# Experts' stage of an attention-and-experts kernel: its batches' front work spread over three batches

## The reference, cut to what matters

```python
x = layernorm(x + (seq_out + gated * mem_val) @ out_w.T + out_b)
logits = x @ gate_w.T + gate_b                  # 10 columns, 8 true experts, 2 null
weights, selected = top_k(softmax(logits), 2)
norm_w = weights of true experts, divided by their sum
combine_w = norm_w scattered over 8 experts
out = sum_e combine_w[:, e] * (x @ expert_w[e] + expert_b[e])
x = layernorm(x + out)
```

## Time and profile before

| | before |
|---|---|
| times of three runs, us | 965.98, 979.03, 979.47; median 979.03 |
| profiled execution: span from first to last instruction, us | 971.7 |
| mean granted TensorE clock in it (1.0 is full) | 0.888 |
| PE busy, share of the span | 814.0 us, 84% |
| DVE busy | 649.2 us, 67% |
| POOL busy | 461.3 us, 47% |
| ACT busy | 346.1 us, 36% |

### The profile page before, as it was taken

The page is one execution under the profiler, slowest core; times in us unless marked ns, Lnnn a source line. Parts: engine busy times, 40 slices in busy tenths (PEclk is TensorE's granted clock), DMA queues, the critical chain, the costliest instruction groups (busy, mean ns, idle before and its releaser), DMA issues.

```text
span 971.7 us, 15580 instructions
## 1 busy us (share of the span) xinstructions
PE 814.0 (84%) x4564; PEld 546.8 (56%) x4564; DVE 649.2 (67%) x1482; ACT 346.1 (36%) x677; POOL 461.3 (47%) x357
## 2 busy tenths in 40 slices
PE   6576757998999999999999968977797787979896
PEld 2333434565656555565565534556686566757774
DVE  2115446675777777777776898537868787787875
ACT  2110323454545545455454534532132221312221
POOL 9000826853654646556455551563545434464420
PEclk9786776898999999999999965678898988989898
DMA  8987284544655666646646326020120202202001
GB/s 276 186 214 118 68 111 91 83 111 97 113 137 74 138 116 110 137 70 141 119 78 147 67 38 191 3 87 2 65 87 0 87 1 87 75 11 86 23 1 44
DMA packets 60536, 89.69 MB, mean 92 GB/s; under 512 B 8249, under 2 KB 37457, under 8 KB 60497
## 3 DMA queue, kind: packets, MB, share of 16 engines
q1 hardware_dynamic: 60496, 89.22, 42.0%
HBM read 54.85 MB, written 33.82 MB: 91 GB/s over the span
## 4 chain that ended last, share of the span: by engine, by line
PE 50%; DVE 17%; DMA 10%; issue 8%; POOL 8%; ACT 3%; SPq 2%; DVEq 0%; POOLq 0%; ACTq 0%
PE ps L1227 13%; PE ps L373 8%; PE ps L337 8%; PE ps L326 7%; PE ps L313 6%; DMA Q<-MT 5%; DVE nmax L464 3%; PE ps L314 3%; DMA qk_scratch<-HL 2%; PE ps L1193 2%; DVE idx L1285 2%; DMA Wm<-mem_scratch 2%; DVE hot L1288 2%; ACT X L1213 1%; DMA Pr<-xT 1%
## 5 line engine op out<-in xcount | busy, mean ns | idle before, releaser
L464 DVE TENSOR_REDUCE nmax<-ps 128x1 f32<-128x384 f32 (+3 forms) x384 | 218.1, 589 | 117.7 <-PE ps L314 117.5
L407 ACT ACTIVATE Pr<-ps 128x512 f32<-128x512 f32 (+2 forms) x384 | 194.8, 528 | 162.8 <-PE ps L326 155.9
L326 PE MATMUL ps<-Q,K 98*128 98x256 f32 (+2 forms) x512 | 189.4, 413 | 37.1 <-DMA Q<-MT 31.7
L313 PE MATMUL ps<-K,Q 96*128 96x256 f32 (+2 forms) x512 | 179.9, 383 | 21.0 <-DVE nmax L464 19.6
L647 POOL TENSOR_SCALAR_AFFINE_SELECT Pr<-Pr 128x512 f32<-128x512 f32 x128 | 87.4, 688 | 225.5 <-ACT Pr L407 223.5
L1227 PE MATMUL ps<-ew_hi,XT 128*128 128x512 f32 x512 | 184.8, 423 | 0.0
L1351 DVE SCALAR_TENSOR_TENSOR A<-ps,cw,A 128x256 f32<-128x256 f32 x256 | 123.6, 483 | 55.9 <-PE ps L1227 45.6
L326 PEld LDWEIGHTS ps<-Q,K 98*128 98x128 f32 x512 | 96.5, 210 | 101.2 <-ACT Pr L407 38.3
L313 PEld LDWEIGHTS ps<-K,Q 96*128 96x128 f32 x512 | 109.5, 214 | 32.4 <-DVE nmax L464 28.2
L314 PE MATMUL ps<-mask_qk,ident_bf 128*128 128x128 bf16 x512 | 125.8, 246 | 0.0
L1227 PEld LDWEIGHTS ps<-ew_hi,XT 128*128 128x128 f32 x512 | 103.6, 202 | 22.1
(11 more groups left out here) (180 smaller groups left out, 1233.1 us busy)
## 6 DMA issues: line engine op xcount, KB each, us to landing
qk_scratch<-HL SPq DMA_DIRECT2D x32, 512.0 KB, 3.1
Q<-qk_scratch SPq DMA_DIRECT2D x96, 128.0 KB, 3.9
K<-qk_scratch SPq DMA_DIRECT2D x96, 128.0 KB, 5.7
Pr<-xT SPq DMA_DIRECT2D x8, 512.0 KB, 9.5
xraw<-xT SPq DMA_DIRECT2D x8, 512.0 KB, 6.3
mem_scratch<-Rl SPq DMA_DIRECT2D x16, 256.0 KB, 6.7
mv_scratch<-MV SPq DMA_DIRECT2D x32, 128.0 KB, 1.7
Wm<-mem_scratch SPq DMA_DIRECT2D x16, 256.0 KB, 10.1
```

Of the source, the lines that this page charges most:

```text
L313: nc.tensor.matmul(o, Q[0:STACK, hh, P * i:P * i + P], K[0:STACK, hh, 0:n], start=True, stop=False)
L326: last = nc.tensor.matmul(o, K[0:STACK + 2, hh, P * kt:P * kt + P], Q[0:STACK + 2, hh, T - n:T], start=True, stop=True)
L407: nc.scalar.activation(probs(g % 2, kt, heads[0], len(heads)), src, ACT.Exp, scale=SCALE).then_inc(s_exp, 1)
L464: nc.vector.tensor_reduce(dst, src, AX_X, ALU.max, negate=True).then_inc(s_max, 1)
```

## The change

The front of a batch is spread over two batches of units instead of one. During the units of batch b, what is called near is done for batch b + 1: turns 2 and 3 after units 3 and 4, logits after unit 6, gating on DVE after combination 6, turning of the weights after unit 13 (its DVE copy after combination 12). What is called far is done for batch b + 2: turns 0 and 1 after units 9 and 10, the projection after units 12 and 13, dve_sums after combination 13, act_norm1 at the end of ACT's list, pool_inputs, turned 0 and 1 and root1 at the end of POOL's. The *_rest functions do the far part of batch 1 ahead of batch 0. Batch 6 has no far part, batch 7 neither. sp_batch is unchanged.

```diff
--- before.py
+++ after.py
@@ -1363,61 +1363,66 @@
             nc.vector.tensor_scalar(ve2[:, par], mv2[:, par, :, 1], EPS, None, ALU.add).then_inc(s_v2, 1)
 
 
-    def pe_batch(pe, b, par, front=True, first=False):
+
+
+
+    def pe_batch(pe, b, par, near=True, far=True, first=False):
         for v in range(UN):
             if v in (0, 2):
                 pe_biases(pe, b, v // 2, par)
             if not (first and v < 3):
                 pe_experts(pe, b, v, par)
-            if front:
-                if v in (0, 1, 8, 9):
-                    pe_turn(pe, b + 1, (0, 1, 8, 9).index(v), 1 - par)
+            if near:
                 if v in (3, 4):
-                    pe_out(pe, b + 1, v - 3)
-                if v == 11:
+                    pe_turn(pe, b + 1, v - 1, 1 - par)
+                if v == 6:
                     pe_logits(pe, b + 1, 1 - par)
-                if v == 14:
+                if v == 13:
                     pe_turn_weights(pe, b + 1)
-
-    def act_batch(act, b, par, front=True, first=False):
+            if far:
+                if v in (9, 10):
+                    pe_turn(pe, b + 2, v - 9, par)
+                if v in (12, 13):
+                    pe_out(pe, b + 2, v - 12)
+
+    def act_batch(act, b, par, near=True, far=True, first=False):
         act_biases(act, b, 0, par)
-        if front:
-            act_turned(act, b + 1, 0, 1 - par)
-            act_turned(act, b + 1, 1, 1 - par)
         act_biases(act, b, 1, par)
-        if not first:
-            act_norm2(act, b - 1, 1 - par)
-        if front:
-            act_norm1(act, b + 1, 1 - par)
+        if near:
             act_turned(act, b + 1, 2, 1 - par)
             act_turned(act, b + 1, 3, 1 - par)
             act_gap(act, b + 1)
-
-    def dve_batch(dve, b, par, front=True):
+        if not first:
+            act_norm2(act, b - 1, 1 - par)
+        if far:
+            act_turned(act, b + 2, 0, par)
+            act_turned(act, b + 2, 1, par)
+            act_norm1(act, b + 2, par)
+
+    def dve_batch(dve, b, par, near=True, far=True):
         for v in range(UN):
             dve_combine(dve, b, v, par)
-            if front:
-                if v == 4:
-                    dve_sums(dve, b + 1, 1 - par)
-                if v == 11:
+            if near:
+                if v == 6:
                     dve_gating(dve, b + 1, 1 - par)
-                if v == 13:
+                if v == 12:
                     dve_turned_weights(dve, b + 1, 1 - par)
-
-    def pool_batch(pool, b, par, front=True, first=False, more=True):
+            if far and v == 13:
+                dve_sums(dve, b + 2, par)
+
+    def pool_batch(pool, b, par, near=True, far=True, first=False):
         pool_base(pool, b, 0, par)
-        if front:
-            pool_turned(pool, b + 1, 0, 1 - par)
-            pool_turned(pool, b + 1, 1, 1 - par)
         pool_base(pool, b, 1, par)
+        if near:
+            pool_turned(pool, b + 1, 2, 1 - par)
+            pool_turned(pool, b + 1, 3, 1 - par)
         if not first:
             pool_root2(pool, b - 1, 1 - par)
-        if front:
-            pool_root1(pool, b + 1)
-            pool_turned(pool, b + 1, 2, 1 - par)
-            pool_turned(pool, b + 1, 3, 1 - par)
-        if more:
+        if far:
             pool_inputs(pool, b + 2)
+            pool_turned(pool, b + 2, 0, par)
+            pool_turned(pool, b + 2, 1, par)
+            pool_root1(pool, b + 2)
 
     def sp_batch(sp, b, par, first=False, more=True):
         if more:
@@ -1471,7 +1476,10 @@
         pool_turned(pool, 0, 2, 0)
         pool_turned(pool, 0, 3, 0)
         pool_inputs(pool, 1)
-        pairs(pool, pool_batch, first=True, before=dict(more=False), end=dict(front=False, more=False))
+        pool_turned(pool, 1, 0, 1)
+        pool_turned(pool, 1, 1, 1)
+        pool_root1(pool, 1)
+        pairs(pool, pool_batch, first=True, before=dict(far=False), end=dict(near=False, far=False))
         pool_root2(pool, NB - 1, 1)
 
     def act_beside(act, g, u):
@@ -1495,7 +1503,10 @@
         act_turned(act, 0, 2, 0)
         act_turned(act, 0, 3, 0)
         act_gap(act, 0)
-        pairs(act, act_batch, first=True, end=dict(front=False))
+        act_turned(act, 1, 0, 1)
+        act_turned(act, 1, 1, 1)
+        act_norm1(act, 1, 1)
+        pairs(act, act_batch, first=True, before=dict(far=False), end=dict(near=False, far=False))
         act_norm2(act, NB - 1, 1)
 
     def dve_beside(dve, g, u):
@@ -1523,7 +1534,8 @@
         dve.wait_ge(s_pz, 2)
         dve_gating(dve, 0, 0)
         dve_turned_weights(dve, 0, 0)
-        pairs(dve, dve_batch, end=dict(front=False))
+        dve_sums(dve, 1, 1)
+        pairs(dve, dve_batch, before=dict(far=False), end=dict(near=False, far=False))
 
     def pe_beside(pe, g, u):
         if (g, u) == (2, 6):
@@ -1542,10 +1554,14 @@
         pe.wait_ge(s_pl, 3 + NP)
         for v in range(3):
             pe_experts(pe, 0, v, 0)
-        pe_turn_weights(pe, 0)
         for used, n in ((a["s_oc"], a["outs"]), (a["s_on"], a["outs"])):
             pe.wait_ge(used, n)
-        pairs(pe, pe_batch, first=True, end=dict(front=False))
+        pe_turn(pe, 1, 0, 1)
+        pe_turn(pe, 1, 1, 1)
+        pe_turn_weights(pe, 0)
+        pe_out(pe, 1, 0)
+        pe_out(pe, 1, 1)
+        pairs(pe, pe_batch, first=True, before=dict(far=False), end=dict(near=False, far=False))
 
     return {"sync": dict(weights=sp_weights, inputs=sp_inputs, second=lambda sp: sp_load(sp, 1), rest=sp_rest),
             "gpsimd": dict(inputs=pool_first_inputs, turned=pool_first_turned, rest=pool_rest),
```

## The result

| | before | changed |
|---|---|---|
| runs, us | 965.98, 970.89, 979.03, 979.47 | 988.48, 990.31, 991.21, 995.37 |
| median, us | 974.96 | 990.76 |
| span of the profiled execution, us | 971.7 | 986.8 |

The changed kernel takes 1.023 times as long (95% interval 1.018 to 1.028). The profiled execution's span of 986.8 is a device time of 988.48: 1.7 us lie around it, not the 7.3 that I had read out of the median.

The account below looks back on a forecast made before the run. TensorE was taken as bound, waiting 6.65 us a batch for a gating slowed by GpSimd. Six batches +7.9, ends +0.4 and +7.0 gave +15.3: span 987.0, plus 7.3 around it, 994 us; range 974 to 1008.

Parts of the forecast that it names:

- 15.3: Whole span: growth in us, summed from +7.9 for six batches, +0.4 before them and +7.0 behind the last logits.
- 0.9 + 2.5 - 1.5: One batch, logits to logits: longer gating wait, new wait before the second bias matmuls, X1 wait gone, in us.
- rival A: Gating: the subtractions of turned 0 and 1 don't hold it; a batch 2.0 us lower, 981 us; chance 0.15.
- The gating's wait is taken over by the banks: TensorE before unit 11: waits for combination 7 behind the gating, 7.6 us against 6.65 before, +0.9 a batch.
- The two subtractions: GpSimd's turned 0 and 1, now beside the gating: taken to hold it by 2.6 us, making it 12.6 us.
- Norm1 ahead of the biases: Before unit 2: the second bias matmuls wait for the chain sums, root1, norm1, bias copy; +2.5 us a batch.
- X1's wait gone: Before turn 2: norm1 is done a batch ahead, so TensorE's wait for X1 goes; -1.5 us a batch.
- rival C: Behind the new wait before unit 2: TensorE's clock falls, 1.3 to 2.5 us a batch, 1002 to 1009 us; chance 0.25.
- the slow stretch behind the gating's wait stays: TensorE behind the gating's wait: same kind of wait, a little longer, so the lower-clock stretch there stays; no size added.
- The ends: Outside the six batches: +0.4 us to batch 1's first logits, +7.0 behind the last logits for five more units.
- GpSimd's order and VectorE's load: pool_inputs starts about 1.1 us before the gating; VectorE is loaded 35.8 of 42 us a batch, so not the bound.
- the gating is long because of GpSimd: VectorE's gating: 10.6 us, waiting instruction by instruction for GpSimd's pool_inputs; about 4.2 in the last batch.

Follow-up runs that it names:

- experiment 2: The changed kernel, with GpSimd held until the gating's end before the subtractions of turned 0 and 1 of two batches ahead; 1.000 of before (0.995 to 1.005).
- experiment 1: The changed kernel, with the far act_norm1 moved behind both bias copies of the next batch; 1.002 of before (0.998 to 1.007).
- experiment 4: The kernel before, with pool_inputs cut after its first addition and the other three steps held until the gating's end; 0.959 of before (0.952 to 0.966).

## Why the prediction was right, and where not

The span came out at 986.8 against 987.0 and the median at 990.76 against 994. That close a hit is luck in good part. The stage grew by 18.7 us, not 15.3; the earlier arrival (3.6 us) and the too large margin around the span (5.6) hid it.

The 15.3 hold a slip of mine. A batch was to grow by 0.9 + 2.5 - 1.5 = 1.9 us, which is 11.4 in six. I added the 1.9 to the one batch of 40.4 us and compared six of the sum with 245.9, which is six of 41.0, and so wrote 7.9; rival A has the same slip. Put right, my terms give 18.8 for the stage. That it is what was measured is luck again, since the terms behind it differ. In the six batches I had 11.4 us of waits and nothing for the clock. The rows have 11.7, of which 2.3 are waits (before the turning of the weights 37.6 us, now before unit 11 35.0; for X1 7.7, gone; for the bias copy 12.6, new) and 9.4 are TensorE's busy time for the same 1010 instructions (200.55 and 209.99, at mean granted clocks of 0.91 and 0.86).

Against the median of before that the comparison used, the change is 2.3%, a little beyond the 2% on whose near side I had put most of the chance.

- **The gating's wait is taken over by the banks**: right in kind, wrong in its sign. TensorE was held from the logits to unit 11 for 13.26 us in the batch shown (808.54 to 821.80) against 13.9 reckoned: 7.0 uncovered, not 7.6. But the 6.65 of before, which I called a wait, are a wait of 4.87 and 1.8 us that the units behind the logits took longer at the lower clock (0.50 of full, in the row below), and this batch had the shortest of the six waits (4.9 to 8.3 us). Over the six the wait fell from 37.6 to 35.0 us, 0.4 less a batch, where I had +0.9. The two subtractions held the gating for 2.0 us (experiment 2), not 2.6: they ran 2.54 for both, and one step of VectorE got in beside each. The first of the six gatings took only 9.3. The row, of the kernel before (borders, length, PE busy, granted clock, DMA share, GB/s), lies in the units behind the logits:

```profile
811.30:814.30 3.00, 3.00 (x9) 0.50 0.00 0
```

- **Norm1 ahead of the biases**: right, 2.1 us a batch against 2.5, and 6.8 at batch 0, where my times implied about as much; experiment 1 shows that it was this edge.
- **X1's wait gone**: right; it had been 1.3 us on average, not 1.5.
- **The clock**: rival C came true beside the forecast. Behind the 2 us wait for the bias copy, units 2 and 3 took 4.1 to 4.4 us instead of 2.8 in five of six batches. That is about 1.5 us in each, 7.6 in all, most of the 9.4 us by which TensorE's busy time grew; without the bias waits (experiment 1) that time is back at 200.3. I gave C 0.25 and kept it out of the sum; the step that failed is "the slow stretch behind the gating's wait stays", as if the only slow stretch were that one. That one too was longer in the batch shown: at the lower clock units 11 and 12 took 5.3 us (821.80 to 827.09), where before it was 3.2 us for the turning and one unit (821.24 to 824.46).
- **The ends**: +1.0 to the first logits (0.4 expected) and +6.0 behind the last (7.0 expected).
- **GpSimd's order and VectorE's load**: right; pool_inputs started 1.3 us before the gating (1.1 expected), and VectorE waited for TensorE at the weights' copy (15.2 us in seven), as one does that is no bound.

The base of the argument, that the gating is long because of GpSimd, was shown four ways: thin steps (4.2 to 4.6 us), held steps in the kernel before (0.959), held subtractions (-2.0 us), and cut steps in the changed one (4.2 to 4.6 us). The Trainium skill (SBUF — State Buffer, on the shared port pair) names the cause: one of the two engines holds the second pair of ports for a whole instruction. The runs agree in its pattern: VectorE's two-input steps end with GpSimd's instructions, and its combinations, one operand of which is in PSUM, run their 1.00 us beside them. Single-input steps are held too: the cast that makes idx took 1.81 us at 812.25 in the changed kernel and 0.17 in experiment 4. The runs don't show the port itself.

The change moved the gating to where it could have been hidden, and left beside it what makes it long. With that moved too, the same structure is the fastest kernel of the study.

What stays open: where the other 1.8 of TensorE's 9.4 us lie, and why one of six waits of 2.2 us (before 797.64) left the clock full and five of 1.8 to 2.3 did not. Filling that wait with other TensorE work was not tried.

## What to carry to other kernels

Before making room around a slow step, compare its instructions with the same ones where the neighbour engine is idle: if they differ tenfold, move the neighbour, not the step. Reckon a gain or a loss over all batches: the one that I chose had the shortest wait of six, and a time at the lower clock looked like a wait. When work is moved a batch ahead, look at what its last step now precedes on its own engine: a short copy behind it may be what the bottleneck engine needs first. And read a stage by its own borders when what runs ahead of it varies as much as the effect.

## What the runs showed of the hardware

Small VectorE instructions of 0.17 us (those with two inputs in SBUF, CAST and TENSOR_SCALAR) took up to 2.4 us when a GpSimd instruction on 1024 columns was under way, and about 1.1 beside one on 512. The gating's MAX8, FIND_INDEX8 and MEMSET kept their 0.38, 0.16 and 0.06 us there. TensorE's granted clock fell behind waits of only 1.8 to 2.3 us in five batches: 0.61 of full over 840.7 to 844.7, a mix of its two levels (1.2 and 2.4 GHz), where another batch (797.6 to 800.8) stayed at 1.00.
